# Issuing the next half's normalised input, q and k earlier inside a step of a fused window-attention kernel

## The reference, cut to what matters

```python
# x: (8, 128, 32, 32) float32
# 1. window attention: 8x8 windows (64 tokens), 8 heads of 16 channels
win = windows(x)                                   # (B*16, 64, 128)
q, k, v = split(layernorm(win) @ in_w.T + in_b)
o = softmax(q @ k.T / 4) @ v
y = win + o @ out_w.T + out_b
# 2. feed-forward with residual
y = y + silu(layernorm(y) @ fc1_w.T + fc1_b) @ fc2_w.T + fc2_b
# 3. attention without softmax over the 1024 tokens of an image, E = 64
k, v = wk @ y + bk, y @ wv.T + bv
out = wo @ ((q @ k) / 1024 @ v) + bo + y           # folded into one 128x128 matrix per image
```

## Time and profile before

| | |
|---|---|
| median of 3 runs | 377.72 us (377.37 to 381.28) |
| the profiled execution's own time | 377.23 us |
| its span, first to last instruction | 375.4 us |
| busy share of the span: PE, DVE, ACT, POOL | 93%, 78%, 64%, 45% |
| granted TensorE clock, mean | 0.991 of full speed |
| one even and one odd step in the middle | 18.89 us and 23.45 us |

### The profile page before, as it was taken

The page is one execution under the profiler, slowest core; times in us unless marked ns, Lnnn a source line. Parts: engine busy times, 40 slices in busy tenths (PEclk is TensorE's granted clock), DMA queues, the critical chain, the costliest instruction groups (busy, mean ns, idle before and its releaser), DMA issues.

```text
span 375.4 us, 9822 instructions
## 1 busy us (share of the span) xinstructions
PE 349.0 (93%) x3349; PEld 294.9 (79%) x3349; DVE 294.3 (78%) x863; ACT 241.7 (64%) x438; POOL 167.2 (45%) x176
## 2 busy tenths in 40 slices
PE   3679999999999999999999999999999999999764
PEld 2567788888888888888888888888888888878552
DVE  8387889798788878898788878898798878687452
ACT  1426677774969478784969478684969478664540
POOL 6353054644455434645455434635455434431420
PEclk9999999999999999999999999999999999999898
DMA  4133140403122121403122121403122120300101
GB/s 126 34 88 81 33 109 9 113 2 82 60 77 63 41 70 56 111 1 77 63 76 64 38 74 56 109 3 77 63 72 68 35 77 31 86 2 18 40 1 56
DMA packets 31570, 21.94 MB, mean 58 GB/s; under 512 B 22272, under 2 KB 23360, under 8 KB 31552
## 3 DMA queue, kind: packets, MB, share of 16 engines
q1 hardware_dynamic: 31552, 21.71, 21.1%
HBM read 4.92 MB, written 4.19 MB: 24 GB/s over the span
## 4 chain that ended last, share of the span: by engine, by line
PE 76%; DVE 6%; issue 4%; ACT 2%; POOL 1%; DVEq 0%; POOLq 0%; ACTq 0%
PE p_scoreT L634 12%; PE p_c L529 11%; PE p_score L611 9%; PE p_attn L649 9%; PE p_a L529 6%; PE p_scoreT L629 4%; PE p_a L593 4%; PE p_c L707 3%; PE p_d L529 3%; DVE xn_tok L1105 3%; PE p_c L678 2%; PE p_d L719 2%; PE p_a L577 2%; PE p_a L567 2%; PE p_c L684 2%
## 5 line engine op out<-in xcount | busy, mean ns | idle before, releaser
L910 ACT ACTIVATE probs<-p_scoreT 128x512 f32<-128x512 f32 x64 | 38.6, 603 | 35.1 <-PE p_scoreT L634 34.6
L465 POOL TENSOR_TENSOR hid_l<-hid,hid_h 128x512 fp32r<-128x512 f32 x30 | 40.3, 1364 | 43.5 <-ACT hid_h L944 41.6
L611 PE MATMUL p_score<-kd_h,qd_h 128*128 128x128 f32 (+1 forms) x512 | 54.4, 249 | 0.9 <-DVE row_max L1158 0.8
L611 PEld LDWEIGHTS p_score<-kd_h,qd_h 128*128 128x128 f32 (+1 forms) x512 | 50.0, 163 | 5.9 <-DVE row_max L1158 2.4
L649 PEld LDWEIGHTS p_attn<-vd,probs 128*64 128x64 f32 x1024 | 36.2, 139 | 22.2 <-issue 15.1
L470 POOL TENSOR_TENSOR y_l<-y,y_h 128x512 fp32r<-128x512 f32 (+1 forms) x17 | 20.5, 1208 | 69.4 <-ACT y_h L924 69.4
L1158 DVE TENSOR_REDUCE row_max<-p_score 128x8 f32<-128x512 f32 x64 | 43.9, 687 | 6.7 <-PE p_score L611 6.7
L649 PE MATMUL p_attn<-vd,probs 128*64 128x34 f32 x1024 | 45.7, 245 | 2.7 <-ACT probs L910 2.7
L457 POOL TENSOR_SCALAR kd_l<-k_l,head_a 128x512 fp32r<-128x512 f32 x16 | 26.7, 1669 | 33.5 <-DVE k_l L1140 19.8
L634 PE MATMUL p_scoreT<-qd_h,kd_h 128*128 128x256 f32 x128 | 41.3, 322 | 0.0
L449 POOL TENSOR_TENSOR rstd<-rstd,minus_half 128x4 f32<-128x4 f32 (+1 forms) x33 | 35.5, 1076 | 2.8
(11 more groups left out here) (183 smaller groups left out, 877.9 us busy)
## 6 DMA issues: line engine op xcount, KB each, us to landing
x_in<-in_x SPq DMA_DIRECT2D x16, 256.0 KB, 2.9
qd_h<-q_h SPq DMA_DIRECT2D x64, 64.0 KB, 2.0
qd_l<-q_l SPq DMA_DIRECT2D x64, 64.0 KB, 2.0
vd<-v_tok SPq DMA_DIRECT2D x64, 64.0 KB, 2.2
out<-out_sb SPq DMA_DIRECT2D x16, 256.0 KB, 2.1
fc_rows<-in_L_conv_fc_w SPq DMA_DIRECT2D x2, 128.0 KB, 2.5
in_w_rows<-in_L_conv_in_w SPq DMA_DIRECT2D x1, 192.0 KB, 2.7
out_w_rows<-in_L_conv_out_w SPq DMA_DIRECT2D x1, 64.0 KB, 2.4
```

The source lines that it names most:

```text
L465: pool.tensor_tensor(hid_l[:, t], hid[:, t], hid_h[:, t].bitcast(F32), ALU.subtract).then_inc(hid_low[t], 1)
L611: last = pe.matmul(p_score[0:rows, 2 * KEYS * j:2 * KEYS * (j + 1)], qd_h[:, h.par, j, 2 * KEYS * p:2 * KEYS * p + rows], kd_h[:, h.par, 2 ...
L910: act.activation(probs[:, p % 2], p_scoreT[:].rearrange("row (win j q) -> row win j q", win=2, j=QUADS), ACT.Exp, scale=SCORE_SCALE).then_ ...
```

## The change

No instruction is added or taken away; three engines issue some of them at another place of the step.

- **PE**: `a_q` goes from behind `c_yT` to directly behind `b_score(2)`, ahead of `c_fc2` and `b_attn(0)`. `a_k` takes the old place of `a_q`, ahead of `c_kv`; its own old place ahead of `b_attn(1)` is empty.
- **ScalarE**: `a_xn` of the next half is issued at the end of the step before, ahead of the load of the exponential's table instead of behind it. `a_q` goes ahead of `c_y2`, `a_k` and `a_k_block(0)` ahead of `b_exp(1)`, `a_k_block(1)` right behind it.
- **VectorE**: `a_xn` goes ahead of `c_y1` and `b_max(2)`, `a_q` ahead of `c_y2`, `a_k` ahead of `c_kv` and `b_max(3)`.

```diff
 # PE, step
                 b_score(b, 2)
+                if with_a:
+                    a_q(a)
                 if with_tail:
                     c_fc2(tail)
                 b_attn(b, 0)
                 if with_c:
                     c_yT(c)
                 if with_a:
-                    a_q(a)
+                    a_k(a)
                 if with_tail:
                     c_kv(tail)
...
-                if with_a:
-                    a_k(a)
                 b_attn(b, 1)
 # ScalarE, step
                 load_exp_table(b)
-                if with_a:
-                    a_xn(a)
...
                 if not with_last:
                     c_o(b)
+                if with_next:
+                    a_xn(next_a)
 # VectorE, step
                 b_widen(b, 1)
+                if with_a:
+                    a_xn(a)
                 if with_c:
                     c_y1(c)
```

More of the change, by code:

```diff
@@ L970, in prologue @@
                 a_v(a)
+                a_xn(loop.half(1))
             def step(loop, b, with_a, with_next, with_c, with_tail, with_d, with_last=False):
@@ L981, in step @@
                 if with_a:
-                    a_q(a)
+                    a_k(a)
+                    a_k_block(a, 0)
                 b_exp(b, 1)
                 if with_a:
-                    a_k(a)
-                    a_k_block(a, 0)
+                    a_k_block(a, 1)
                     a_v(a)
@@ L992, in step @@
                     c_o(Part(loop, 0))
-                if with_a:
-                    a_k_block(a, 1)
                 if with_d:
```

## The result

The changed kernel takes **383.44 us** (median of 4 runs, 382.12 to 383.53) against 377.55 for the kernel before (4 runs beside it, 377.09 to 381.28): a ratio of **1.013, 95% interval 1.0076 to 1.0183** (it weighs all the runs; the two medians alone give 1.016, since one of the four runs before took 381.28). The profiled execution took 382.12 us, 380.3 of it span, against 377.23 and 375.4: +4.9.

What follows compares the result with a forecast made beforehand. TensorE's list was taken to set the pace, with nothing to win in the rearranged stretch. New waits, less 0.4 in step 1, summed to +6.2 us on 377.23: 383.4, with 0.49 for the median 383.9; range 380.0 to 388.5.

Steps and rivals of the forecast that it cites:

- What costs nothing: Same matmuls with their turns, ScalarE's moved `a_xn` and SP's unchanged list: priced at zero, nil to 0.1 us if ScalarE isn't free.
- Term A: TensorE's earlier `a_q` waits for VectorE's `xn_l`: 0.39 us in even steps, 0.17 in odd ones.
- Term B: Without `a_k` as cover, `b_attn(1)` waits for `b_exp(1)`: 0.12 us in even steps, nil in odd ones.
- Term C: `y2` and `kv_tok` come late on VectorE: zero wait at `c_kv`, 0.35 us at `d_kvT` in odd steps.
- Step 0: First step, with `a_q` ahead of `b_attn(0)` like the even steps: given the same 0.4 us of cost.
- Step 1: Step without `c_fc2`: `a_q` fills TensorE's 0.60 of idle time at `b_attn(0)`, with a small wait, so -0.4 us.
- The sum: Seven even steps 3.4 us, six odd ones 2.8, first step 0.4, second -0.4: together +6.2 us on 377.23, 383.4.
- step lengths near 19.4 and 23.9: Sign that the forecast is right: lengths of the even and the odd step in the profile after.
- Faster: Rival: VectorE brings the next half's statistics forward, `a_back`'s 0.4 wait goes in 7 odd steps: 374.5 us; chance 0.05.
- Hidden after all: Rival: `xn_l` reaches TensorE without a wait, only Term B and half of Term C remain: 380.4 us; chance 0.18.
- `c_kv` waits too: Rival: VectorE's and ScalarE's chain is 0.3 us slower, `y2` comes late, 13 steps pay 0.25 each: 387.2; chance 0.11.
- The cast behind `kd_l`: Rival: `b_widen(3)` waits for POOL's `kd_l`, next statistics start 0.9 later, `a_back` waits 0.7 more: 388.1 us; chance 0.10.

Runs made afterwards that it cites:

- a4: The kernel before with only ScalarE's `a_xn` moved ahead of the exponential's table load: 378.10 us, ratio 1.0012.
- a1: The changed kernel with VectorE's `a_xn` one place earlier, ahead of `b_widen(1)`: 380.27 us, ratio 1.0079.
- a2: The changed kernel with VectorE's `a_xn` one place later, behind `c_y1`: 393.81 us, ratio 1.0427.
- b4: b3 with, in even steps, `c_kv` behind `b_score(3)` on PE and behind `b_max(3)` on VectorE, `a_q` there behind `b_norm(0)`: 375.43 us, ratio 0.996.
- a3: The changed kernel with `a_k` back at its old place on all three engines, only input and q moved: 390.78 us, ratio 1.0351.
- b1: a3 with VectorE's `c_y2` put back ahead of `a_q`: 384.67 us, ratio 1.0187.
- c1: The changed kernel with VectorE's `c_kv` put back ahead of `a_k`: 381.05 us, ratio 1.0098.
- c2: The changed kernel with VectorE's `c_y2` put back ahead of `a_q`: 382.46 us, ratio 1.0119.
- b2: The changed kernel with step 0 in its old order on all three engines, ScalarE's `a_xn` staying moved: 382.34 us, ratio 1.0115.
- b3: The changed kernel with step 0 in old order and, on VectorE, `a_xn` ahead of `b_widen(1)`, `c_y2` of `a_q`, `c_kv` of `a_k`: 376.64 us, ratio 0.9981.

## Why the prediction came out as it did

**The forecast was 383.9, and 383.44 was measured.** The likeliest case is the one that happened: the same matmuls, and new waits in TensorE's list. But the total is nearer than its terms are.

**What costs nothing** held, on ScalarE (a4) and, for the turns, in the even step: 0.35 + 0.12 of waits less 7.84 - 7.41 = 0.43 leaves 0.04 for the turns, where I had written 0.08 for turns that get smaller at `c_fc2` and `b_attn(0)` and 0.05 back for the others.

**Term A** held in size: 0.35 for 0.39 in even steps, 0.15 for 0.17 in odd ones. a1 and a2 move it both ways. **Term B**: the start 0.85 behind `b_score(3)` is the one I had worked out, so the 0.12 is there as far as the 0.73 under both is right. No run takes this wait away alone; b4 got 0.05 of it back.

**Term C** was the right mechanism with the wrong size. `y2` came 0.3 ahead of `c_kv`, so zero was right, and a3 shows how little cover that is. `kv_tok` started 11.70 behind the start of the step (217.96 - 206.26), where I had 11.99 (213.51 - 201.52), so 0.35 of wait became 0.20. At `d_kvT` I had a start 1.26 us later than before (0.91 and 0.35); measured from `b_score(2)` it is 7.72 against 6.64 (with `b_score(2)` 0.63 ahead of 206.93), so 1.08. The term of the sum that was mis-sized more was the one behind it. I let `a_k` leave its place for 0.80, the price of the same matmuls in `a_q`'s place, and took the turn as unchanged. In the kernel before, `d_kvT` to `b_attn(1)` took 1.96 (212.94 to 214.90) and now takes 0.95: 1.01, the turns included. Together the odd step grew by 0.08 (23.51 against 23.43) instead of 0.46. Six steps: 0.43 us instead of 2.8.

**Step 0** I had taken to be like the even steps, 0.4. TensorE stood for 1.33 at `a_q`. In b1, where the clock stayed at 1.00 with that same wait (1.34), step 0 took 17.04, 0.44 more than before: the wait took the place of the one for `b_exp(0)`, and without a fall of the clock the step costs about what I had put. In c1, with the list of the kernel after, TensorE also waits 0.38 at `b_attn(1)` of this step, which b1 doesn't. So I put 1.3 to 1.7 us of the 2.10 down to the clock (an estimate: 18.70 - 17.04, with and without those 0.38). That was in none of my cases.

**Step 1**: the gain of 0.4 did not come. `a_q` did fill the idle time at `b_attn(0)`, but the new wait at `b_attn(1)`, 0.44, took it back. I had priced ScalarE's order only where `a_xn` moved, not where `b_exp(1)` went behind `a_k`. In later steps TensorE has `c_kv` to do meanwhile: in the even step ScalarE is through with `kd_h` 0.25 before `b_exp(1)` can start, so its new order costs nothing there.

**The sum** for steps 0 to 14 was +6.2 and is +5.53: 2.94 for 3.4, 0.43 for 2.8, 2.10 for 0.4, 0.06 for -0.4. An error of 2.4 us in the odd steps and one of 1.7 in step 0, with opposite signs, cancelled for the most part, and that was luck. So was the rest: the profiled execution came out at 382.12 where I had 383.4, and the median lay 1.32 above it where I had put 0.49. The line "step lengths near 19.4 and 23.9" was right for the first and wrong for the second. Of the waits that I had asked the profile for, it names only the one on `xn_l`, with 0.19 for 0.35; the other two show in the starts.

**The rivals.** *Faster*: `a_back`'s wait didn't change, 1.10 for 1.09 from the start of the step. With all the waits hidden (b4) it is still there. *Hidden after all* did not happen, since `xn_l` made TensorE wait; its 0.3 for half of C was too much as well, with C at 0.35. *`c_kv` waits too* did not happen, but stood 0.3 us away. *The cast behind `kd_l`* did in part. POOL and DVE at the end of the even step, which answer to the earlier trace rows:

```profile
201.10 1.57 POOL L457 TENSOR_SCALAR kd_l<-k_l,head_a 128x512 fp32r<-128x512 f32 x1
```

```profile
201.19 0.88 DVE L1170 CAST max_wide<-row_max 128x512 bf16<-128x512 f32 x1
202.15 0.89 DVE L1089 BATCH_NORM_STATS2 stats<-p_a 128x6 f32<-128x128 f32 x4
```

The cast started 0.09 behind `kd_l` and took 0.88 instead of 0.42, yet it ended at 202.07 and `kd_l` at 202.67: it lost 0.46, and it did not wait for POOL's end. The Trainium skill, "SBUF — State Buffer", "Who interferes with whom", has whoever issues first keep the ports for the whole instruction; this row doesn't agree with it as the whole story, though POOL's spans are rough. The loss isn't a fixed factor either: in the even steps of a1, of the kernel after and of b4 the cast starts 0.06, 0.09 and 0.29 behind `kd_l` and takes 0.91, 0.88 and 0.68, so it ends 0.97 behind `kd_l`'s start each time.

I had also read too little in the kernel before. Its odd step has a cast that started well behind `kd_l`, took 0.78 and ended 0.28 behind it:

```profile
216.67 1.57 POOL L457 TENSOR_SCALAR kd_l<-k_l,head_a 128x512 fp32r<-128x512 f32 x1 [2.03 <-issue]
```

```profile
217.74 0.78 DVE L1169 CAST max_wide<-row_max 128x512 bf16<-128x512 f32 x1
```

And where the cast was at its shortest, 0.42 in the even step, it was `kd_l` that took 1.84 instead of 1.57. So the two get in each other's way in the trace before too, as far as these rows tell, against what I wrote of it. The 0.46 more was paid out of the 0.51 that the statistics waited before: they still start 0.64 behind `a_transpose`, as before, so it cost nothing.

**What stays open** is why the clock falls in step 0. In the seven executions with `a_q` early there it fell some 0.2 to 1.1 us behind the start of `a_q` in four (after, a2, a3, c1, with waits of 1.33 and 1.34), before `a_q` in two (a1, c2) and not at all in b1, with a wait of 1.34; in the five without it (before, a4, b2, b3, b4) it did not fall. That is one execution of each, and b1 to b4 ran on one chip, where it fell in none. I tried nothing on this that would tell.

## What to carry to other kernels

When the bound engine has no idle time, a reordering that leaves its work alone can lose much and win only what the turns between groups give (0.3 us in the odd step here): price each moved consumer by its producer's place in the *other* engines' lists, and look at what those engines' heads now wait for, since an early instruction that waits (here `q_l` for `q_h`) makes everything behind it late. Move the producer on the side engine far enough ahead of its consumer, and nothing with a long wait ahead of work that others need: nearly the same order of matmuls was 1.3% slower with one order on VectorE and 0.2% faster with another (b3). And price the first steps, where half the usual work is missing, by their own rows: here they held 2.1 of the 5.5 us, and a lower clock came with most of that.

## What the runs showed of the hardware

- In step 0 the granted clock fell to 0.50 and stayed there for some 3 us in six of twelve profiled executions; by the estimate above it cost 1.3 to 1.7 us in the kernel after. In four of the six an idle time of 1.33 or 1.34 us at `a_q` had just ended. But idle times of 1.34 (b1), 1.24 (a1), 1.03 (a4, b3, b4), 1.02 (b2), 1.01 (c2) and 0.95 (before) in that step were not followed by a fall, and in a1 and c2 it fell during the matmuls behind one of 0.78 or 0.79, which all twelve have.
- The tail behind step 14, where TensorE is often idle, took 45.7 us with the clock at 0.50 for some 3 us of it (after) and 47.6 with some 14 us of it (b2), though little changed there. A difference of a microsecond between kernels is read from the steps, not from the whole time.
- The same group of three 512-column matmuls costs 0.75 to 1.01 us by what stands around it: 1.01 between `d_kvT` and `b_attn(1)`, 0.75 between `b_score(2)` and `c_fc2` (run b3, 206.63 to 207.38). `d_kvT` and `b_attn(1)`, both of narrow tiles, follow each other in 0.95 where `d_kvT` to a wide matmul takes 1.07.
- A VectorE cast that starts 0.06 to 0.29 us behind GpSimd's `kd_l` takes 0.68 to 0.91 us instead of 0.42 and ends 0.97 behind `kd_l`'s start; one that starts 0.07 behind a `kd_l` of 1.84 instead of 1.57 takes its 0.42.
